# One of three products of a graph layer, moved from the node stage into the scoring stage

## The chip, the cores and the metric

The kernel runs on 1 core of one Trainium2 chip. The metric is device time in microseconds of one execution, the median of several runs. Everything is float32.

## What is computed

Four graph layers over 50,000 nodes and 50,000 edges, 256 features. Every layer begins with `h = relu(layernorm(x))`. The change lies in the third one:

```python
h = jnp.maximum(_layernorm(x, axis=-1), 0.0)
x = x + _L2_gnn_ref(h, src, dst, W_s, W_t, W_attn, W_fc, b_fc)

proj_s = feature @ W_s.T                 # feature is h
proj_t = feature @ W_t.T
z = proj_s[src] + proj_t[dst]
z = jnp.where(z >= 0, z, NEG_SLOPE * z)
e = (z @ W_attn.T)[:, 0]
... softmax of e over the edges of one source gives alpha
msg = feature[src] * alpha[:, None]
agg = jax.ops.segment_sum(msg, dst, num_segments=n)
return agg @ W_fc.T + b_fc
```

The kernel multiplies by `W_fc` first: `h @ W_fc.T` for every node goes to memory as the table `h2`, and the last stage of the layer gathers rows of `h2` and sums them. So three products leave the node stage: by `W_s` (table `from_src`), by `W_t` (`to_dst`) and by `W_fc` (`h2`).

## The kernel before

The program is a row of stages, each a `Phase` that ends in a barrier of all engines. Of the third layer three stages matter here.

**The node stage** (`node_pass`, layer 2) walks 50,176 padded rows in 98 groups of 4 tiles of 128 rows. For a group: SyncE loads x (L1208); VectorE adds two biases (L1282, L1283), takes mean and variance (L1304, L1308, L1311) and normalizes (L1318); GpSimd takes the inverse root (L1353) and also scatters the sorted source keys (L1361 to L1366, four indirect DMAs); TensorE turns a tile by two transposes (L1413); ScalarE rectifies it into `h_t` (L1463); TensorE multiplies the turned tile by the 768 columns of `w2` (L1435: 512 columns into one PSUM tile, 256 into another, and each float32 product over two halves of the 256 features); ScalarE copies both to `out` (L1481, L1482); SyncE stores four tables (L1229): `from_src`, `to_dst`, `h2` and `own2`, 512 KB each.

Each engine runs its own list of steps, software-pipelined by `pipeline`: a step with lag L works on group c-L in turn c. On VectorE normalize (lag 2) stands ahead of average (lag 0); on SyncE the load (lag 0) stands ahead of the stores (lag 6). Buffers exist for S = 4 groups, so the join of group c waits until all four stores of group c-4 have landed (L1281, semaphore `t_put`). TensorE turns the first tile of the next group before it multiplies the last tile of this one, and that turn waits for `normed` of the next group.

**The scoring stage** (`score_sources`) comes next. GpSimd gathers rows of `from_src` and `to_dst` for every edge (L1555, L1557), two indirect DMAs per tile of 128 edges, 8 in a block of 4 tiles; VectorE adds, bends and reduces them to a score and makes two one-hot operands; TensorE places the score by one matmul per tile (L1613). ScalarE and SyncE have nothing to do in this stage.

**The merge** of the layer follows some stages later and is the first reader of `h2`.

Of the kernel before, what the change touches and what calls it, by code (L numbers as in the profile page):

```python
# [12 lines left out]
P = 128  # L13
U = 8
R = 16
BANKS = 8
D = 256
# [719 lines left out]


def tile_rows(table, base, n=G):

    return table[bass.ds(base, n * P), :].rearrange("(g p) f -> p g f", p=P)
# [398 lines left out]
def node_pass(nc, k, layer, x_in, mixed_in=None, tables=()):  # L1140
# [6 lines left out]
    n_put = len(tables)  # L1147
    n_out = {0: D + 3, 1: 2 * D, 2: 3 * D, 3: P + 8}[layer]
    banks = 2 if layer == 2 else 4

# [17 lines left out]
    minus_half = ph.sb("minus_half", [P, G])  # L1168
    h_t = [ph.sb(f"h_t{n}", [P, D]) for n in range(G)]
    out = both("out", {0: [P, 1, G, D + 3], 1: [P, 1, G, D], 2: [P, 3, G, D], 3: [P, 1, G, P + 8]}[layer])  # L1170
    junk = [ph.sb(f"junk{n}", [P, D]) for n in range(2)]
# [20 lines left out]
    with nc.Block() as block:  # L1192
        @block.sync
        def _(sp):
# [15 lines left out]
            def store_tables(q):  # L1210

                if layer == 0:
                    sp.wait_ge(out_made, q.H + 1)
                    parts = [rows_h[q.h][:], pair_h[q.h][:]]
                elif layer == 1:
                    sp.wait_ge(out_made, G * (q.H + 1))
                    sp.sem_inc(turn_sp, 1)
                    sp.wait_ge(raw_made, G * (q.H + 1))
                    parts = [out[q.h][:, 0], own[q.h][:]]
                elif layer == 2:  # L1220
                    sp.wait_ge(out_made, G * (q.H + 1))
# [183 lines left out]
        def _(pe):  # L1405
# [11 lines left out]
            def work(q):  # L1417
# [3 lines left out]
                for g in range(G):  # L1421
# [11 lines left out]
                    for w, (n, matrix) in enumerate(k.products[layer]):  # L1433
                        for c in range(2):
                            ins = nc.tensor.matmul(p_out[w][g % banks][:, 0:n], h_t[g][:, c * P:(c + 1) * P], matrix[:, c, :],  # L1435
                                                   start=c == 0, stop=c == 1)
# [4 lines left out]
        def _(act):  # L1441
# [16 lines left out]
            def rectify(q, g):  # L1458
                t = G * q.H + g
                act.wait_ge(turned, t + 1)  # L1460
                if not q.first:
                    act.wait_ge(product, t - G + 1)
                nc.scalar.activation(h_t[g][:], p_turn[g % 2][:, 0:D], ACT.Relu).then_inc(rectified, 1)  # L1463

            def work(q):
# [3 lines left out]
                for g in range(G):  # L1469
# [10 lines left out]
                    if layer == 2:  # L1480
                        nc.scalar.copy(out[q.h][:, 0:2, g, :], p_out[0][g % banks][:].rearrange("p (n f) -> p n f", n=2))  # L1481
# [32 lines left out]
    ph.close()  # L1514
def score_sources(nc, k, table_src, table_dst, out):

# [10 lines left out]
    at_high = [ph.sb(f"at_high{n}", [P, NT]) for n in range(HOT)]  # L1527
    p_table = ph.ps("table", [P, 512])
    indexed, turn_pool, digits, added, bent, scored, low_hot, high_hot, placed, s_done = (ph.sem(n) for n in (
        "indexed", "turn_pool", "digits", "added", "bent", "scored", "low_hot", "high_hot", "placed", "done"))  # L1530
# [10 lines left out]
    with nc.Block() as block:  # L1541
# [65 lines left out]
        def _(pe):  # L1607
            def tiles(i, first, n):
                for j in range(n):
# [335 lines left out]
def gnn_kernel(nc, a, out, check=None):  # L1945
# [11 lines left out]
    with ExitStack() as ctx:  # L1957
# [15 lines left out]
        def early(name, shape, dt=F32):  # L1973
# [14 lines left out]
        h1, from_src, to_dst, h2, h3 = (dram(n, (k.NP, w)) for n, w in  # L1988
                                        (("h1", D), ("from_src", D), ("to_dst", D), ("h2", D), ("h3", P + 8)))
        mix0, own1, x2, own2, x3 = (dram(n, (k.NP, D)) for n in ("mix0", "own1", "x2", "own2", "x3"))  # L1990

# [36 lines left out]

        node_pass(nc, k, 2, x2, tables=(from_src, to_dst, h2, own2))
        hold = Phase(nc, "soft2")  # L2030
# [9 lines left out]
        score_sources(nc, k, from_src, to_dst, by_place)  # L2040
        shares_by_source(nc, k, by_place, shares)
# [40 lines left out]
```

## Time and profile before

| | us |
|---|---|
| median of 3 runs | 9786.06 |
| lowest, highest | 9783.69, 9792.57 |
| the profiled execution | 9778.72 |
| its span, first to last instruction | 9777.0 |
| node stage of the third layer, in the trace | 4515.6 to 5637.8 |
| scoring stage, in the trace | 5639.1 to 6783.9 |

The profile is one execution. Its engines are PE (TensorE matmuls), PEld (its weight loads), DVE (VectorE), ACT (ScalarE), POOL (GpSimd) and SP (SyncE, which here only issues DMAs). Over the whole span PE is busy 62%, DVE 58%, POOL 50%, ACT 32%; such averages mix stages with different limits, so the stages are read one by one. A float32 matmul of the program stands in the trace as two records.

### The profile page before, as it was taken

The numbers are of one execution on the slowest core, as the hardware profiler recorded it, in microseconds if no ns is written. First come the engines' busy times: TensorE is split into PE (matmuls) and PEld (weight loads), VectorE is DVE, ScalarE is ACT, GpSimd is POOL, SyncE is SP. The second block draws the span as 40 slices with busy tenths as digits, with TensorE's granted clock in tenths as the row PEclk, the third lists the DMA queues.
The fourth block names the chain that finished last, engine by engine and source line by source line (L and its number), as shares of the span: only waits on it lengthen the run. The fifth ranks groups of instructions, "written<-read, shape, count | busy, mean of one in ns | idle before, by whom it ended". The sixth has DMA issues, their size and how long they took to land. (4 is left out here: it accounts for less than half of the span.)

```text
span 9777.0 us, 155051 instructions
## 1 busy us (share of the span) xinstructions
PE 6076.9 (62%) x21338; PEld 3661.3 (37%) x21339; DVE 5653.9 (58%) x19482; ACT 3099.9 (32%) x10799; POOL 4876.5 (50%) x5997
## 2 busy tenths in 40 slices
PE   4666877756768887677999945444003678500277
PEld 3554233324543433455666611111002557400165
DVE  4666988873558776354445455555001458755664
ACT  2665022211554443254444400000000466411046
POOL 1333177756632212664444467775666652455252
PEclk8998577777989998799999966666556999755599
DMA  2332000004876654596666632332002797411057
GB/s 84 134 132 96 0 1 1 1 1 151 284 256 215 214 206 173 181 302 233 236 234 234 222 98 90 91 90 66 1 0 76 234 302 217 144 42 42 23 178 229
DMA packets 779248, 1347.62 MB, mean 138 GB/s; under 512 B 139839, under 2 KB 546391, under 8 KB 779156
## 3 DMA queue, kind: packets, MB, share of 16 engines
q1 hardware_dynamic: 208564, 650.10, 19.0%
q10 hardware_dynamic: 413792, 410.91, 13.2%
q0 software_dynamic: 156800, 285.65, 10.5%
q8 instruction: 25, 0.41, 0.0%
q14 instruction: 67, 0.55, 0.0%
HBM read 751.95 MB, written 594.32 MB: 138 GB/s over the span
## 5 line engine op out<-in xcount | busy, mean ns | idle before, releaser
L1435 PE MATMUL node_p_out<-w,node_h_t 128*128 128x512 f32 (+3 forms) x7840 | 2614.7, 466 | 379.1 <-ACT node_h_t L1463 141.9
L990 PE MATMUL merge_banks<-merge_rows,merge_mask 128*128 x6264 | 1680.7, 425 | 744.0 <-SPq L959 464.5
L1435 PEld LDWEIGHTS node_p_out<-w,node_h_t 128*128 128x128 f32 x7840 | 1357.1, 197 | 1077.7 <-issue 734.9
L990 PEld LDWEIGHTS merge_banks<-merge_rows,merge_mask 128*128 128x128 f32 x6264 | 1278.1, 211 | 1146.6 <-issue 954.0
L972 DVE TENSOR_SCALAR merge_mask<-ramp,dst_at,soft_at_step 128x128 f32<-128x128 f32 x2349 | 847.2, 366 | 1069.8 <-PE merge_banks L990 950.3
L1078 POOL DMA_INDIRECT merge_rows<-h,merge_take_i x1176 | 1125.1, 957 | 655.6 <-issue 249.4
L1022 ACT COPY merge_total<-merge_banks 128x256 f32<-128x256 f32 x1568 | 577.6, 369 | 1251.5 <-PE merge_banks L990 1135.4
L1613 PE MATMUL score_table<-score_at_high,score_at_low 128*128 128x392 f32 x784 | 565.6, 827 | 588.8 <-DVE score_at_high L1574 584.0
L1009 ACT COPY merge_banks<-merge_held 128x256 f32<-128x256 f32 x1568 | 588.1, 376 | 897.5 <-DMA merge_held<-own 643.3
L1353 POOL TENSOR_TENSOR node_inv_std<-node_var,node_minus_half 128x4 f32<-128x4 f32 x392 | 437.0, 1115 | 751.0 <-DVE node_var L1311 750.0
L1463 ACT ACTIVATE node_h_t<-node_p_turn 128x256 f32<-128x256 f32 x1568 | 594.7, 385 | 349.6 <-PE node_p_turn L1413 344.9
L1413 PE MATMUL node_p_turn<-ident,node_xn 128*128 128x128 f32 x3136 | 625.3, 282 | 107.6 <-DVE node_xn L1318 103.8
L1413 PEld LDWEIGHTS node_p_turn<-ident,node_xn 128*128 128x128 f32 x3136 | 439.6, 145 | 444.6 <-issue 232.4
L1613 PEld LDWEIGHTS score_table<-score_at_high,score_at_low 128*128 128x128 f32 x784 | 183.3, 291 | 970.8 <-DVE score_at_low L1588 970.4
L455 POOL DMA_INDIRECT rank_src_of_src<-ends,rank_src_take_src x392 | 371.2, 947 | 340.9 <-ACT rank_src_take_dst L435 228.7
L1660 POOL DMA_INDIRECT score_a<-h,score_take_a x392 | 370.1, 944 | 287.1 <-ACT score_take_a L1636 165.0
L1366 POOL DMA_INDIRECT src_sorted<-node_key,node_key_at x392 | 397.7, 1015 | 179.8 <-issue 94.6
L1375 POOL TENSOR_TENSOR node_small<-node_small,node_half 128x4 f32<-128x4 f32 x98 | 98.8, 1008 | 775.4 <-ACT node_junk L1450 775.4
L1557 POOL DMA_INDIRECT score_b<-to_dst,score_take_b x392 | 413.8, 1056 | 130.3 <-issue 130.3
L1555 POOL DMA_INDIRECT score_a<-from_src,score_take_a x392 | 389.7, 994 | 168.9 <-issue 89.6
L1125 POOL DMA_INDIRECT share_in_got<-shares,share_in_take_i x392 | 372.5, 950 | 170.2 <-issue 79.3
L1585 DVE TENSOR_TENSOR score_z<-score_a,score_b 128x256 f32<-128x256 f32 x392 | 163.9, 418 | 494.9 <-DMA score_b<-to_dst,score_take_b 494.9
(409 smaller groups left out, 9678.3 us busy)
## 6 DMA issues: line engine op xcount, KB each, us to landing
h<-node_out SPq DMA_DIRECT2D x196, 512.0 KB, 5.7
merge_held<-own ACTq DMA_DIRECT2D x196, 512.0 KB, 5.8
x<-merge_total ACTq DMA_DIRECT2D x196, 512.0 KB
node_x<-x SPq DMA_DIRECT2D x196, 512.0 KB, 5.9
node_x<-in_x SPq DMA_DIRECT2D x194, 512.0 KB
h<-node_rows_h SPq DMA_DIRECT2D x98, 512.0 KB, 2.7
merge_held<-h ACTq DMA_DIRECT2D x98, 512.0 KB
mix<-merge_total ACTq DMA_DIRECT2D x98, 512.0 KB
```

What stands on the lines that cost most here:

```text
L972: ins = nc.vector.tensor_scalar(mask[j][:], k.ramp[:, 0:P], columns(k.dst_at, s), columns(weight, s), ALU.is_equal, ALU.mult)
L990: nc.tensor.matmul(banks[:, bass.ds(nc.s_assert_within(at[2 * j + 1], 0, (BANKS - 1) * 512, skip_runtime_bounds_check_because=small), D)], ...
L1009: nc.scalar.copy(bank(q, g), held[q.h][:, g, :]).then_inc(seeded, 1)
L1022: nc.scalar.copy(total[q.h][:, g, :], bank(q, g)).then_inc(kept, 1)
L1078: nc.gpsimd.indirect_dma_start(rows[:, (j + n) * D:(j + n + 1) * D], None, table, bass.IndirectOffsetOnAxis(take_i[:, j + n:j + n + 1], 0) ...
L1353: nc.gpsimd.tensor_tensor(inv_std[q.h][:], var[q.h][:], minus_half[:], ALU.pow).then_inc(std_made, 1)
L1366: nc.gpsimd.indirect_dma_start(k.src_sorted, bass.IndirectOffsetOnAxis(key_at[:, g:g + 1], 0), key[:, g:g + 1], None, bounds_check=k.NP - ...
L1413: ins = nc.tensor.transpose(p_turn[g % 2][:, c * P:(c + 1) * P], xn[q.h][:, g, c * P:(c + 1) * P], k.ident[:])
L1435: ins = nc.tensor.matmul(p_out[w][g % banks][:, 0:n], h_t[g][:, c * P:(c + 1) * P], matrix[:, c, :], start=c == 0, stop=c == 1)
L1463: nc.scalar.activation(h_t[g][:], p_turn[g % 2][:, 0:D], ACT.Relu).then_inc(rectified, 1)
L1557: nc.gpsimd.indirect_dma_start(b[m][:], None, table_dst, bass.IndirectOffsetOnAxis(take_b[:, m:m + 1], 0)).then_inc(got[j // LAG], 16)
L1613: nc.tensor.matmul(p_table[:, 0:NT], at_low[j % HOT][:], at_high[j % HOT][:], start=first and j == 0, stop=False, skip_group_check=True).t ...
```

## The change

- In the node stage the product by the last 256 columns of `w2` goes, and its copy. `out` has two parts instead of three, and the PSUM tiles freed make four banks for the 512-column product instead of two.
- The rectified turned tiles, which lived in four small buffers, are now written into `kept_t`, one of 512 KB for each of the 4 group slots, and the fourth store of a group writes `kept_t` to a new table `turned2` in place of the store of `h2`. Before the first tile of a slot ScalarE waits for that slot's earlier stores.
- In the scoring stage SyncE loads a group of `turned2` (lag 0), TensorE multiplies one tile by the 256 columns right behind each placing matmul, ScalarE copies the result, and SyncE stores a group of `h2` (lag 3). The stage ends when those stores have landed.

```diff
-    n_out = {0: D + 3, 1: 2 * D, 2: 3 * D, 3: P + 8}[layer]
-    banks = 2 if layer == 2 else 4
+    n_out = {0: D + 3, 1: 2 * D, 2: 2 * D, 3: P + 8}[layer]
+    banks = 4
...
+    if layer == 2:
+        kept_t = both("kept_t", [P, G, D])
...
-                    parts = [out[q.h][:, n] for n in range(3)] + [biased[q.h][:]]
+                    parts = [out[q.h][:, n] for n in range(2)] + [biased[q.h][:]]
...
+                if layer == 2:
+                    sp.dma_start(turned_group(tables[3], q.H), kept_t[q.h][:].rearrange("p g f -> p (g f)")
+                                 ).then_inc(t_put[q.h], 16)
...
-                if not q.first:
+                if layer == 2:
+                    if not q.new and g == 0:
+                        act.wait_ge(t_put[q.h], 16 * n_put * q.i)
+                elif not q.first:
                     act.wait_ge(product, t - G + 1)
-                nc.scalar.activation(h_t[g][:], p_turn[g % 2][:, 0:D], ACT.Relu).then_inc(rectified, 1)
+                nc.scalar.activation(turned_rows(q.h, g), p_turn[g % 2][:, 0:D], ACT.Relu).then_inc(rectified, 1)
...
-                        nc.scalar.copy(out[q.h][:, 2, g, :], p_out[1][g % banks][:, 0:D]).then_inc(out_made, 1)
...
+                    side, g = j // G, j % G
+                    if g == 0:
+                        pe.wait_ge(h_got[side], 16 * (i + 1))
+                    if not (first and side == 0):
+                        pe.wait_ge(h_made, t - G + 1)
+                    for c in range(2):
+                        ins = nc.tensor.matmul(p_h[g][:, 0:D], h_t[side][:, g, c * P:(c + 1) * P],
+                                               k.w2[:, c, 2 * D:3 * D], start=c == 0, stop=c == 1)
+                    ins.then_inc(product, 1)
...
+                    if g == 0 and not first:
+                        act.wait_ge(h_put[side], 16 * i)
+                    act.wait_ge(product, i * R + j + 1)
+                    nc.scalar.copy(h[side][:, g, :], p_h[g][:, 0:D]).then_inc(h_made, 1)
...
+            def load(q):
+                if not q.new:
+                    sp.wait_ge(product, G * q.last)
+                sp.dma_start(h_t[q.h][:].rearrange("p g f -> p (g f)"), turned_group(turned_in, q.H)).then_inc(h_got[q.h], 16)
+            def store(q):
+                sp.wait_ge(h_made, G * q.H + G)
+                sp.dma_start(group_rows(h_out, q.H * ROWS), h[q.h][:]).then_inc(h_put[q.h], 16)
+            pipeline(sp, groups, [(0, load), (3, store)], apart=2)
...
-                      2: [(2 * D, k.w2[:, :, 0:2 * D]), (D, k.w2[:, :, 2 * D:3 * D])], 3: [(P + 8, k.w3)], 4: []}
+                      2: [(2 * D, k.w2[:, :, 0:2 * D])], 3: [(P + 8, k.w3)], 4: []}
```

TensorE in the node stage, before, the last two tiles of a group (`p_turn` is the turned tile, `xn` the normalized rows of a slot, `p_out0` and `p_out1` the products of 512 and 256 columns):

```order
L1413 MATMUL node2_p_turn1<-ident,node2_xn0 128x128 x2
L1435 MATMUL node2_p_out0_0<-w2,node2_h_t2 128x512 x2
L1435 MATMUL node2_p_out1_0<-w2,node2_h_t2 128x256 x2
L1413 MATMUL node2_p_turn0<-ident,node2_xn1 128x128 x2
L1435 MATMUL node2_p_out0_1<-w2,node2_h_t3 128x512 x2
L1435 MATMUL node2_p_out1_1<-w2,node2_h_t3 128x256 x2
```

The turn of the next slot's first tile (`xn1`) stands ahead of the product of this group's last tile (`h_t3`).

The same engine and place now:

```order
L1429 MATMUL node2_p_turn1<-ident,node2_xn2 128x128 x2
L1443 REGISTER_ALU
L1448 REGISTER_ALU
L1451 MATMUL node2_p_out0_0<-w2,node2_kept_t2 128x512 x2
L1429 MATMUL node2_p_turn0<-ident,node2_xn2 128x128 x2
L1443 REGISTER_ALU
L1448 REGISTER_ALU
L1451 MATMUL node2_p_out0_1<-w2,node2_kept_t2 128x512 x2
```

The two 256-column matmuls of each tile are gone, and the turned operand is the kept one.

TensorE in the loop of the scoring stage, before (`table` collects the scores):

```order
L1613 MATMUL score2_table<-score2_at_high0,score2_at_low0 128x392
L1611 REGISTER_ALU
L1613 MATMUL score2_table<-score2_at_high1,score2_at_low1 128x392
L1611 REGISTER_ALU
L1613 MATMUL score2_table<-score2_at_high2,score2_at_low2 128x392
```

One placing matmul follows the other, each behind its wait.

The same place now (`h_t1` is a loaded group, `p_h` the product):

```order
L1638 MATMUL score2_table<-score2_at_high1,score2_at_low1 128x392
L1646 MATMUL score2_p_h1<-w2,score2_h_t1 128x256 x2
L1636 REGISTER_ALU
L1638 MATMUL score2_table<-score2_at_high2,score2_at_low2 128x392
L1646 MATMUL score2_p_h2<-w2,score2_h_t1 128x256 x2
```

The two 256-column matmuls stand behind each placing matmul.

SyncE in the loop of the node stage, before, from the load of one group to the wait ahead of the next:

```order
L1208 DMA node_x<-x 128x1024
L1221 ISA
L1229 ISA
L1229 DMA from_src<-node_out 128x1024
L1229 DMA to_dst<-node_out 128x1024
L1229 DMA h<-node_out 128x1024
L1229 DMA own<-node_biased 128x1024
L1207 REGISTER_ALU
```

The four stores of a group stand behind one load, `own` last. The same engine and place now:

```order
L1221 DMA node_x<-x 128x1024
L1234 ISA
L1242 ISA
L1242 DMA from_src<-node_out 128x1024
L1242 DMA to_dst<-node_out 128x1024
L1242 DMA own<-node_biased 128x1024
L1244 ISA
L1244 DMA turned<-node_kept_t 128x1024
L1220 REGISTER_ALU
```

The store of `h` has gone, and one of `turned`, of the same size, stands last.

## Rows read from the trace of the kernel before

**Rows 1.** Busy time by stretch: node stage, scoring stage, an earlier merge.
```profile
4800.00:5200.00 400.00, 400.00 (x1429) 241.61 (x1428) 197.95 (x537) 164.18 (x429) 194.84 (x251) 1.00 0.64 235
5700.00:6200.00 500.00, 251.77 (x347) 81.08 (x347) 285.36 (x1040) 0.00 (x0) 368.18 (x433) 0.66 0.30 91
...
4200.00:4400.00 200.00, 149.48 (x597) 114.52 (x597) 108.18 (x300) 120.73 (x346) 127.68 (x159) 0.96 0.95 309
```

The columns are the stretch, its length in us, and for PE, PEld, DVE, ACT and POOL the busy us (instructions); then TensorE's granted clock as a share of full speed, the share of the DMA engines' time, and GB/s.

**Rows 2.** The 256-column product, node stage: busy us, mean ns, idle before.
```profile
L1435 PE MATMUL node_p_out<-w,node_h_t 128*128 128x256 f32 x1568 | 402.4, 379 | 0.0
```

**Rows 3.** Timeline of one group, node stage: start us, us, instruction, idle before it.
```profile
5099.89 2.75 PE L1435 MATMUL node_p_out<-w,node_h_t 128*128 128x512 f32 x8
...
5102.69 2.75 PE L1435 MATMUL node_p_out<-w,node_h_t 128*128 128x512 f32 x8
...
5103.16 0.38 ACT L1482 COPY node_out<-node_p_out 128x256 f32<-128x256 f32 x1
...
5103.78 0.34 SPq L1229 DMA_DIRECT2D from_src<-node_out  x1
...
5106.91 1.00 SPq L1208 DMA_DIRECT2D node_x<-x  x1
...
5110.92 1.23 DVE L1282 TENSOR_TENSOR node_xc<-node_x,own_bias 128x1024 f32<-128x1024 f32 x1 [5.55 <-DMA own<-node_biased]
...
5114.98 0.33 SPq L1229 DMA_DIRECT2D from_src<-node_out  x1
...
5115.28 1.38 DVE L1318 TENSOR_SCALAR node_xn<-node_xc,node_moments,node_inv_std 128x256 f32<-128x256 f32 x4
```

**Rows 4.** Timeline of the second layer's node stage, whose product has 512 columns.
```profile
3204.84 1.88 PE L1435 MATMUL node_p_out<-w,node_h_t 128*128 128x512 f32 x4
...
3206.78 1.88 PE L1435 MATMUL node_p_out<-w,node_h_t 128*128 128x512 f32 x4
```

**Rows 5.** Half-microsecond stretches of the node stage, columns as in rows 1.
```profile
5106.00:5106.50 0.50, 0.50 (x3) 0.26 (x2) 0.00 (x0) 0.50 (x3) 0.04 (x1) 1.00 1.00 401
...
5111.50:5112.00 0.50, 0.50 (x3) 0.23 (x2) 0.50 (x1) 0.50 (x3) 0.00 (x0) 1.00 0.42 126
```

**Rows 6.** Waits of DVE in the node stage: total us, times, longest.
```profile
DVE node_xc L1282 <- DMA own<-node_biased: 501.2, 94, 6.3
```

**Rows 7.** POOL in one group of the node stage, timeline: first and last instruction.
```profile
5104.21 1.19 POOL L1353 TENSOR_TENSOR node_inv_std<-node_var,node_minus_half 128x4 f32<-128x4 f32 x1 [3.81 <-DVE node_var L1311]
...
5110.39 0.97 POOL L1366 DMA_INDIRECT src_sorted<-node_key,node_key_at  x1 [0.30 <-issue]
```

**Rows 8.** The scatters of POOL in the node stage, all of them.
```profile
L1366 POOL DMA_INDIRECT src_sorted<-node_key,node_key_at x392 | 397.7, 1015 | 179.8 <-issue 94.6 <-POOL node_key L1362 85.2
```

**Rows 9.** POOL in the scoring stage, groups of instructions.
```profile
L1557 POOL DMA_INDIRECT score_b<-to_dst,score_take_b x392 | 413.8, 1056 | 130.3 <-issue 130.3
L1555 POOL DMA_INDIRECT score_a<-from_src,score_take_a x392 | 389.7, 994 | 168.9 <-issue 89.6 <-POOL score_take_b L1551 79.3
```

**Rows 10.** Waits of DVE in the scoring stage.
```profile
DVE score_z L1585 <- DMA score_b<-to_dst,score_take_b: 494.9, 98, 11.3
```

**Rows 11.** One-microsecond stretches of the scoring stage, columns as in rows 1.
```profile
6206.00:6207.00 1.00, 0.00 (x0) 0.00 (x0) 0.27 (x1) 0.00 (x0) 0.88 (x1) 0.50 0.05 16
...
6210.00:6211.00 1.00, 1.00 (x2) 0.38 (x2) 1.00 (x6) 0.00 (x0) 0.91 (x1) 0.50 0.44 131
...
6213.00:6214.00 1.00, 0.89 (x2) 0.30 (x2) 0.31 (x2) 0.00 (x0) 0.70 (x2) 1.00 0.26 94
```

**Rows 12.** Gathers of POOL in the merge at 4200 to 4400 us: ns min/median/max.
```profile
L1078 POOL DMA_INDIRECT merge_rows<-h,merge_take_i x127: 940/946/1032, 4200.1 to 4399.1; - x127
```

**Rows 13.** A gather in the scoring stage's loop, POOL beside busy DVE.
```profile
6223.86 1.30 POOL L1555 DMA_INDIRECT score_a<-from_src,score_take_a  x1 [0.30 <-issue]
```

**Rows 14.** End of the scoring stage, timeline.
```profile
6783.36 0.57 DVE L1604 COPY soft_by_place<-score_table 128x392 f32<-128x392 f32 x1 [1.23 <-PE score_table L1613]
```

**Rows 15.** Landing of the first layer's 512 KB stores.
```profile
DMA to landing us min/median/max: 2.6/2.7/3.3
```

More of the change, by code:

```diff
@@ L736, in pipeline, with turned_group @@
         step(s // S, s % S)
+def turned_group(table, H):
+    return table[bass.ds(H * P, P), :]
 def tile_rows(table, base, n=G):
@@ L1168, in node_pass, with turned_rows @@
     minus_half = ph.sb("minus_half", [P, G])
-    h_t = [ph.sb(f"h_t{n}", [P, D]) for n in range(G)]
-    out = both("out", {0: [P, 1, G, D + 3], 1: [P, 1, G, D], 2: [P, 3, G, D], 3: [P, 1, G, P + 8]}[layer])
+    if layer == 2:
+        kept_t = both("kept_t", [P, G, D])
+    else:
+        h_t = [ph.sb(f"h_t{n}", [P, D]) for n in range(G)]
+    def turned_rows(side, g):
+        return kept_t[side][:, g, :] if layer == 2 else h_t[g][:]
+    out = both("out", {0: [P, 1, G, D + 3], 1: [P, 1, G, D], 2: [P, 2, G, D], 3: [P, 1, G, P + 8]}[layer])
     junk = [ph.sb(f"junk{n}", [P, D]) for n in range(2)]
@@ L1434, in work @@
                         for c in range(2):
-                            ins = nc.tensor.matmul(p_out[w][g % banks][:, 0:n], h_t[g][:, c * P:(c + 1) * P], matrix[:, c, :],
+                            ins = nc.tensor.matmul(p_out[w][g % banks][:, 0:n], turned_rows(q.h, g)[:, c * P:(c + 1) * P], matrix[:, c, :],
                                                    start=c == 0, stop=c == 1)
@@ L1480, in work @@
                     if layer == 2:
-                        nc.scalar.copy(out[q.h][:, 0:2, g, :], p_out[0][g % banks][:].rearrange("p (n f) -> p n f", n=2))
-                        nc.scalar.copy(out[q.h][:, 2, g, :], p_out[1][g % banks][:, 0:D]).then_inc(out_made, 1)
+                        nc.scalar.copy(out[q.h][:, 0:2, g, :], p_out[0][g % banks][:].rearrange("p (n f) -> p n f", n=2)
+                                       ).then_inc(out_made, 1)
                     else:
@@ L1514, in node_pass, with score_sources @@
     ph.close()
-def score_sources(nc, k, table_src, table_dst, out):
+def score_sources(nc, k, table_src, table_dst, out, turned_in, h_out):
     ph = Phase(nc, "score2")
@@ L1528, in score_sources @@
     p_table = ph.ps("table", [P, 512])
+    groups = NT // G
+    h_t = [ph.sb(f"h_t{n}", [P, G, D]) for n in range(S)]
+    h = [ph.sb(f"h{n}", [P, G, D]) for n in range(S)]
+    p_h = [ph.ps(f"p_h{n}", [P, 512]) for n in range(G)]
+    product, h_made = ph.sem("product"), ph.sem("h_made")
+    h_got, h_put = ph.sem_per_slot("h_got", S), ph.sem_per_slot("h_put", S)
     indexed, turn_pool, digits, added, bent, scored, low_hot, high_hot, placed, s_done = (ph.sem(n) for n in (
@@ L1614, in tiles, with _ @@
                                      stop=False, skip_group_check=True).then_inc(placed, 1)
-            in_tiles(pe, tiles)
+                    side, g = j // G, j % G
[7 more added lines that the diff above has]
+                    ins.then_inc(product, 1)
+            in_tiles(pe, tiles)
+        @block.scalar
+        def _(act):
+            def tiles(i, first, n):
+                for j in range(n):
+                    side, g = j // G, j % G
+                    if g == 0 and not first:
+                        act.wait_ge(h_put[side], 16 * i)
+                    act.wait_ge(product, i * R + j + 1)
+                    nc.scalar.copy(h[side][:, g, :], p_h[g][:, 0:D]).then_inc(h_made, 1)
+            in_tiles(act, tiles)
+        @block.sync
+        def _(sp):
+            def load(q):
[6 more added lines that the diff above has]
+            pipeline(sp, groups, [(0, load), (3, store)], apart=2)
+            for side in range(S):
+                sp.wait_ge(h_put[side], 16 * uses_of(side, groups))
     ph.close()
@@ L1989, in gnn_kernel @@
                                         (("h1", D), ("from_src", D), ("to_dst", D), ("h2", D), ("h3", P + 8)))
+        turned2 = dram("turned2", (k.NT // G * P, G * D))
         mix0, own1, x2, own2, x3 = (dram(n, (k.NP, D)) for n in ("mix0", "own1", "x2", "own2", "x3"))
@@ L2027, in gnn_kernel @@
         hold.close()
-        node_pass(nc, k, 2, x2, tables=(from_src, to_dst, h2, own2))
+        node_pass(nc, k, 2, x2, tables=(from_src, to_dst, own2, turned2))
         hold = Phase(nc, "soft2")
@@ L2039, in _ @@
                 nc.vector.memset(by_place[:], 0.0).then_inc(zero, 1)
-        score_sources(nc, k, from_src, to_dst, by_place)
+        score_sources(nc, k, from_src, to_dst, by_place, turned2, h2)
         shares_by_source(nc, k, by_place, shares)
```

## The prediction

> **What bounds the kernel now.** I read the granted clock and busy time by stretch first, then inside the two stages the groups of instructions, the waits, and one group's timeline.
>
> In the node stage TensorE is the bound: in 400 us it is busy 400, at full clock (2.4 GHz), and 1429 records at 40 to a group (4 tiles of 8 product and 2 transpose records) are 35.7 groups, so 11.20 us each [rows 1]. The timeline agrees: stores of one group issue at 5103.78, of the next at 5114.98, and tiles start at 5099.89 and 5102.69, 2.80 us apart [rows 3]. VectorE waits 501.2 us there, 5.3 a group, for the store of `own` to land [rows 6]; that costs nothing as long as TensorE is late anyway. DMA is busy 0.64 of the time [rows 1], or 7.2 us of a group's 11.20.
>
> In the scoring stage GpSimd is the bound. 433 instructions in 500 us at 10 to a block of four tiles are 43.3 blocks, 11.55 us each [rows 1]; 8 of the 10 are gathers of 994 to 1056 ns with about 0.3 us of issue before each [rows 9]. VectorE waits for a gather's data once in every block, 98 times [rows 10]. TensorE is busy half the time at a mean clock of 0.66, DMA 0.30, ScalarE 0 [rows 1].
>
> **The change, node stage.** Removed from each tile: four passes of 256 columns (two matmuls, two records each: 1568 records, 402.4 us of modelled time [rows 2]) and a copy of 0.38 us on ScalarE. What a tile takes without them can be read in the second layer's stage, which has the 512-column product and the same two transposes: starts at 3204.84 and 3206.78, 1.94 us apart [rows 4]. So a tile falls from 2.80 to 1.94, and a group on TensorE from 11.20 to 4 x 1.94 = 7.76 us. 98 groups x 3.44 = 337 us, if nothing else is late.
>
> Something else nearly is: the ring of four slots. Its steps, from the rows of one group [rows 3]: the product of group c-4 ends about 5102.69, its copies end at 5103.54, the first store issues at 5103.78, VectorE starts group c at 5110.92 when `own` has landed (7.14 us after the first issue), and has finished averaging c and normalizing c-1 at 5115.28 + 1.38 = 5116.66 (5.74 us). TensorE then turns group c-1, before its last tile of c-2. That is 13.97 us from product end to normalized. The change takes one copy of 0.38 out of it, 13.6, and I add 0.1 for the signal to TensorE. To the end of the product of c-1 it is then one tile (1.94), four tiles (7.76) and a turn (0.1) more: 23.5 us for three groups, so 7.83 us a group. TensorE's own 7.76 is as good as met.
>
> DMA: the bytes of a group are the same, 5 transfers of 512 KB, since `turned2` takes the place of `h2`, in pieces of the same 4 KB. Stores run at 401 GB/s, and the load behind them is through before 5112, some 8 us after the first issue [rows 3, 5]. About 1 us of that is the start of the first transfer, before which nothing is moved, and the next burst has such a start too, so about 7.2 us of work must fit into 7.83. It does, at 0.92 of capacity instead of 0.64. SyncE issues for 5103.78 to 5107.91, 4.1 us [rows 3], which fits too.
>
> GpSimd: from 5104.21 to 5111.36, 7.15 us a group [rows 7], and the mean scatter of 1015 ns [rows 8] against the 970 shown adds 0.2: 7.4. It fits, with 0.4 to spare. ScalarE's new wait for the slot's stores stands behind one that VectorE has already passed for the same group, and costs nothing; ScalarE had 164 us of work in 143 tiles [rows 1], 1.15 each, and loses 0.38 of it, in a tile of 1.94. The doubled banks only loosen a wait.
>
> Four limits between 7.2 and 7.83 with jitter in each don't give their maximum. The ends are 7.76 (TensorE alone) and 8.8 (GpSimd, below); I take 8.0, close to the measured steps: 98 x (11.20 - 8.0) = 314 us less.
>
> The Trainium skill (GPSIMD Engine Reference, section 1, Specifications) says that GpSimd shares its SBUF interfaces with VectorE and is held up by VectorE's two-port or two-input instructions. The trace bears that out: a gather takes 0.94 us in a merge [rows 12], 1.03 on average in the scoring stage [rows 9] and up to 1.30 where VectorE works [rows 13]. It speaks against this change, since a faster node stage packs VectorE's 5.5 us a group into 8 instead of 11.2.
>
> The skill's page DMA: Bandwidth & Descriptors ("Where 436 GB/s comes from") puts HBM traffic at about 358 GB/s per core. By that the four stores would take 5.9 us instead of 5.2, a third of the difference falls on each group, and the stage would end some 20 us later; the half-microseconds at 401 GB/s [rows 5] speak for the shorter time.
>
> **The change, scoring stage.** Added per tile: four passes of 256 columns on TensorE, which are 2.80 - 1.94 = 0.86 us at full clock and 1.72 at half (1.2 GHz). The placing matmul has two passes of 392 columns; at the same price per column (0.86 us for 1024) that is 0.66, at half clock 1.32. Sum 1.52 or 3.04 us a tile, 6.1 or 12.2 a block against GpSimd's 11.6. The clock is at 0.50 when a burst begins and at 1.00 at its end [rows 11], when TensorE has been busy for a few us; with more work it has less idle time, so the low level will hold for a smaller part. With 4 us of each block at half clock TensorE needs 8 us, and that is hidden. VectorE waits for placings only four tiles back, a whole block, so a TensorE that trails by a tile or two holds nobody.
>
> Queued behind the product's wait for its load are later placings. SyncE loads up to four groups ahead, as each slot is freed, so that wait is over long before. Added on DMA: 1 MB a block, 2.6 us at 400 GB/s beside 3.5 us of gathers, 0.53 of the time. A gather may land later by a transfer, but GpSimd has three blocks of slack before it needs a slot back. ScalarE's copy of 0.4 us a tile and SyncE's two issues a block lie beside idle time. So 0 for the loop; from below 0 too, since nothing of GpSimd's work is taken away.
>
> At the end there is a tail: before, VectorE's copy closes the stage at 6783.93 [rows 14]. Now the last product trails by about 2 us, then a copy of 0.4, the issue, and a landing of 2.7 [rows 15]: +5 us. Later stages read the same tables.
>
> **Sum.** -314 + 5 = -309 us. The profiled execution took 9778.7 and would take 9470; the median of the runs is 9786, which gives 9477.
>
> **The rivals.**
> - *GpSimd or DMA becomes the bound of the node stage.* If each of the four scatters is stretched from 0.97 to the 1.30 of rows 13, GpSimd needs 7.4 + 1.3 = 8.7 to 8.8 us; a DMA ring that never drains would give about the same. For: GpSimd's spare is only 0.4 us, DMA's 0.6. Against: the mean scatter is 1.015. 98 x (11.20 - 8.8) = 235, less the tail 5: 9786 - 230 = 9556. 17%.
> - *TensorE stays at half clock in the scoring stage.* 12.2 us a block instead of 11.6, 98 x 0.6 = 59 us given back: 9536. For: bursts begin at 0.50; against: the clock rises with far less work now. 6%.
> - *The node stage hardly moves,* because the slot ring lengthens with the load on DMA: that would need 3 x 3.3 = 10 us of extra landing. 9786 within 0.2%. Nothing in the rows has it. 2%.
> - *Slower than before: the gathers of the scoring stage pay for the new transfers.* GpSimd is that stage's bound, so each ns on a gather counts 784 times. To eat 309 us each must take 0.39 us more, 1.42 instead of 1.03; at 1.5 us the time would be 9786 - 309 + 784 x 0.47 = 9845. For: DMA load rises from 0.30 to 0.53 and a second queue comes in. Against: at a load of 0.95 [rows 1] gathers take 0.94 us [rows 12]. 4%.
>
> **How the numbers follow.** My forecast, node stage at 7.8 to 8.4 us a group, gets 71%; its own range is 9450 to 9520. The range reported is 9448 to 9570, which takes in the first two rivals. A change within 0.2% (20 us) is about what a measurement of this kernel can't tell from none. Faster by more than that: 71 + 17 + 6 = 94%; within 2%; slower 4%.
>
> **What would show it.** Right: store issues of neighbouring groups in the node stage 7.8 to 8.2 us apart, DMA share about 0.9, TensorE busy over 0.95 at clock 1.00; in the scoring stage GpSimd's gathers at 1.03 us and the span between its ends within 10 us of 1145, TensorE's mean clock above 0.66. Wrong: GpSimd in the node stage waiting for nothing but its own issue, or scatters of 1.2 us (first rival); TensorE without idle time in the scoring stage (second); gathers above 1.1 us there (fourth); VectorE's wait for `own` still over 5 us a group (third).

## The result, and the profile after

The changed kernel takes 9540.05 us, the median of 4 runs (9511.36 to 9549.37), against 9784.88 before: ratio 0.9745, interval 0.9723 to 0.9768, 245 us less. Forecast were 9477 and 309 us less; the range of 9448 to 9570 holds it. The profiled execution took 9511.36, the shortest of the four, 267 us less than the profiled one before.

The two stages by stretch, node stage and scoring stage, in the columns of [rows 1]:

```profile
4700.00:5200.00 500.00, 480.72 (x1459) 223.84 (x1458) 342.45 (x908) 214.95 (x486) 385.89 (x426) 1.00 0.87 318
5400.00:5900.00 500.00, 349.97 (x1025) 236.76 (x1026) 282.06 (x1029) 63.33 (x170) 370.27 (x424) 0.81 0.54 178
```

In the node stage ScalarE now has two records a tile, 486 in 500 us, so 60.75 groups of 8.23 us where [rows 1] gave 11.20. TensorE is busy 0.96 at full clock, DMA 0.87. In the scoring stage TensorE's mean clock rose from 0.66 to 0.81, and GpSimd works off 10 instructions a block as before, 424 in 500 us instead of 433: 11.79 us a block instead of 11.55.

The node stage's store issues, turned groups and VectorE's starts (timeline, answers to [rows 3]):

```profile
5000.20 0.33 SPq L1242 DMA_DIRECT2D from_src<-node_out  x1
...
5007.43 1.23 DVE L1298 TENSOR_TENSOR node_xc<-node_x,own_bias 128x1024 f32<-128x1024 f32 x1 [3.60 <-DMA turned<-node_kept_t]
...
5007.96 0.34 SPq L1242 DMA_DIRECT2D from_src<-node_out  x1
...
5011.79 1.38 DVE L1334 TENSOR_SCALAR node_xn<-node_xc,node_moments,node_inv_std 128x256 f32<-128x256 f32 x4
...
5013.30 0.43 PE L1429 MATMUL node_p_turn<-ident,node_xn 128*128 128x128 f32 x2 [0.40 <-DVE node_xn L1334]
...
5016.34 0.33 SPq L1242 DMA_DIRECT2D from_src<-node_out  x1
```

The stores of two neighbouring groups issue 7.76 us apart where nothing stalls (5000.20 to 5007.96), and 8.38 where TensorE waits for the next group's normalized rows (5007.96 to 5016.34): VectorE could start only when the last store had landed, 7.23 us after the first was issued, ended at 5013.17, and the turn followed at 5013.30. Landing takes as long as before (7.14), though DMA went from 0.64 to 0.87.

Waits of the node stage, total us, times, longest (first two rows VectorE's and TensorE's, the third GpSimd's):

```profile
DVE node_xc L1298 <- DMA turned<-node_kept_t: 215.4, 94, 3.6
...
PE node_p_turn L1429 <- DVE node_xn L1334: 51.2, 47, 22.5
...
POOL node_inv_std L1369 <- DVE node_var L1327: 41.3, 1, 41.3
```

VectorE's wait fell from 5.3 to 2.3 us a group [rows 6]. Such a wait stood after every group before, too, and cost nothing then; that the ring costs time now is said by TensorE, which waits for normalized rows in 47 of 98 groups (before once, at the start). But GpSimd waited for VectorE once in the whole stage, at its start. Its instructions:

```profile
L1382 POOL DMA_INDIRECT src_sorted<-node_key,node_key_at x392 | 403.8, 1030 | 179.8 <-issue 93.1 <-POOL node_key L1378 85.2 <-DVE node_xn L1334 0.9
L1369 POOL TENSOR_TENSOR node_inv_std<-node_var,node_minus_half 128x4 f32<-128x4 f32 x98 | 145.7, 1486 | 42.4 <-DVE node_var L1327 41.3
L1378 POOL COPY node_key<-fields 128x4 f32 x92 | 47.7, 519 | 0.0
```

The scatters hardly changed in this execution (1015 to 1030 ns, [rows 8]), while the inverse root takes 1.49 us and the copy of four keys 0.52 on average. So two limits are met at once, and which binds is what the experiments ask.

The gathers of the scoring stage, and its end (answers to [rows 9, 14]):

```profile
L1582 POOL DMA_INDIRECT score_b<-to_dst,score_take_b x392 | 416.8, 1063 | 130.3 <-issue 124.2 <-DVE score_z L1610 6.1
L1580 POOL DMA_INDIRECT score_a<-from_src,score_take_a x392 | 412.5, 1052 | 168.9 <-issue 89.6 <-POOL score_take_b L1576 79.3
```

```profile
6510.89 0.57 DVE L1629 COPY soft_by_place<-score_table 128x392 f32<-128x392 f32 x1 [3.37 <-PE score_table L1638]
...
6515.96 0.48 DVE L510 MEMSET src_seg_got<- 128x512 f32 x1 [4.50 <-PEq L42]
```

The gathers of `from_src` grew from 994 to 1052 ns, 392 x 0.058 = 23 us, those of `to_dst` from 1056 to 1063, 3 us. From the last gather the end came later too: VectorE waits 3.37 us for the last placing (1.23 before) and 4.50 for the stores of `h2` and the barrier.

The balance of the profiled execution: from VectorE's first row in the node stage to its last copy in the scoring stage 2264.2 us before (4519.7 to 6783.9) and 2002.2 after (4509.3 to 6511.5), 262 less. The node stage gave 98 x (11.20 - 8.21) = 293 (store issues of `own` run from 4530.7 to 5327.0, 97 steps of 8.21). About 30 went back: 26 between the first and the last gather (1131.9 us before, 1158.0 after), 2 from there to the last copy, and the rest between the two loops. The way from that copy to the next stage took 4 more. Another 10 us were gained ahead of the node stage, in stages that the change doesn't touch.

### The profile page after: what moved, and what is told of

Read it like the earlier page. It is cut to its first block and busy times, and to the rows that moved or that the text cites. A ratio compares the mean times of both kernels' runs of the same rounds, so it can differ in the third digit from the quotient of the medians.

```text
span 9509.7 us, 156195 instructions
## 1 busy us (share of the span) xinstructions
PE 5977.7 (63%) x21338; PEld 3705.3 (39%) x21339; DVE 5663.5 (60%) x19482; ACT 3146.4 (33%) x10799; POOL 4992.6 (53%) x5997
## 3 DMA queue, kind: packets, MB, share of 16 engines
q0 software_dynamic: 156800, 285.65, 10.6%
## 5 line engine op out<-in xcount | busy, mean ns | idle before, releaser
L1451 PE MATMUL node_p_out<-w,node_h_t 128*128 128x259 f32 (+2 forms) x4704 | 1531.1, 450 | 379.7 <-ACT node_h_t L1482 139.7
L1451 PEld LDWEIGHTS node_p_out<-w,node_h_t 128*128 128x128 f32 x4704 | 789.8, 201 | 681.3 <-issue 357.8
L1451 PE MATMUL node_p_out<-w,node_kept_t 128*128 128x512 f32 x1568 | 741.5, 595 | 0.0
L1369 POOL TENSOR_TENSOR node_inv_std<-node_var,node_minus_half 128x4 f32<-128x4 f32 x392 | 465.9, 1188 | 389.7 <-DVE node_var L1327 387.6
L1638 PE MATMUL score_table<-score_at_high,score_at_low 128*128 128x392 f32 x784 | 423.9, 630 | 382.4 <-DVE score_at_high L1599 382.4
L1482 ACT ACTIVATE node_h_t<-node_p_turn 128x256 f32<-128x256 f32 x1176 | 437.5, 380 | 322.5 <-PE node_p_turn L1429 317.6
L1580 POOL DMA_INDIRECT score_a<-from_src,score_take_a x392 | 412.5, 1052 | 168.9 <-issue 89.6
L1646 PE MATMUL score_p_h<-w,score_h_t 128*128 128x256 f32 x1568 | 499.9, 451 | 0.0
L1382 POOL DMA_INDIRECT src_sorted<-node_key,node_key_at x392 | 403.8, 1030 | 179.8 <-issue 93.1
L1659 ACT COPY score_h<-score_p_h 128x256 f32<-128x256 f32 x392 | 146.0, 373 | 1040.0 <-PE score_p_h L1646 1040.0
L1582 POOL DMA_INDIRECT score_b<-to_dst,score_take_b x392 | 416.8, 1063 | 130.3 <-issue 124.2
```

The source lines that it names most:

```text
L1369: nc.gpsimd.tensor_tensor(inv_std[q.h][:], var[q.h][:], minus_half[:], ALU.pow).then_inc(std_made, 1)
L1451: ins = nc.tensor.matmul(p_out[w][g % banks][:, 0:n], turned_rows(q.h, g)[:, c * P:(c + 1) * P], matrix[:, c, :], start=c == 0, stop=c == 1)
L1482: nc.scalar.activation(turned_rows(q.h, g), p_turn[g % 2][:, 0:D], ACT.Relu).then_inc(rectified, 1)
L1582: nc.gpsimd.indirect_dma_start(b[m][:], None, table_dst, bass.IndirectOffsetOnAxis(take_b[:, m:m + 1], 0)).then_inc(got[j // LAG], 16)
L1646: ins = nc.tensor.matmul(p_h[g][:, 0:D], h_t[side][:, g, c * P:(c + 1) * P], k.w2[:, c, 2 * D:3 * D], start=c == 0, stop=c == 1)
```

## The experiments

The twelve kernels ran in three batches of four, each on a chip of its own, told apart by the time of the kernel before on it: 10472 us in the first batch, 9785 in the second, 10341 in the third. Ratios are always to the kernel before on the same chip. "The first chip" is below the one of the result, where the kernel before took 9785 us as well.

**node_alone.** The changed node stage with the old scoring stage; the last product is left out, and the merge gathers from another table:

```diff
-        score_sources(nc, k, from_src, to_dst, by_place, turned2, h2)
+        score_sources(nc, k, from_src, to_dst, by_place)
...
-        merge(nc, k, "merge2", own2, x3, table=h2, weight=at_step)
+        merge(nc, k, "merge2", own2, x3, table=from_src, weight=at_step)
```

> The node stage of the changed kernel, with the scoring stage of the one before; the product by the last matrix is left out altogether and the merge gathers from from_src, a table of the same shape, instead. Theory (the node stage gained 98 groups x 3.0 us, the scoring stage gave some 32 us back): about 9785 - 295 = 9490 us, store issues of neighbouring groups 8.2 us apart, gathers of the scoring stage at 994 and 1056 ns as before. Rival (the loss is in the node stage or in later stages, not in the transfers beside the gathers): as the changed kernel, 9510 to 9540.

Measured: 0.9744 (0.9730 to 0.9758), 10208.6 us against 10471.6, 263 us less. That is not comparable with the 0.9745 of the whole change, which was taken on another chip. Stores of `own`, node stage (shortest, median and longest issue in ns, first and last start):

```profile
L1242 SPq DMA_DIRECT2D own<-node_biased x98: 15/738/1982, 5164.7 to 5977.2; - x98
```

97 steps of 8.38 us: the gain of the node stage on this chip is 98 x 2.82 = 277 us. The row of the gathers has 1170 us from first to last with the old scoring stage (5989.5 to 7160.0), where the first chip's profile has 1132, so the stage is slower here by itself. The 9490 us expected were for the first chip and weren't tested. The 8.2 us a group expected, and gathers as before, were missed here: 8.38 us, and 1013 and 1032 ns instead of 994 and 1056.

**score_alone, score_compute, score_transfers.** The old node stage, and beside the old scoring work the new one on x2 with its result in a spare table: all of it; the matmuls and copies alone; the loads and stores alone.

```diff
-        score_sources(nc, k, from_src, to_dst, by_place)
+        score_sources(nc, k, from_src, to_dst, by_place, x2.rearrange("(r g) f -> r (g f)", g=G), spare)
...
# score_compute: no SyncE block, and
-                        ins = nc.tensor.matmul(p_h[g][:, 0:D], h_t[side][:, g, c * P:(c + 1) * P],
+                        ins = nc.tensor.matmul(p_h[g][:, 0:D], k.ident[:],
...
# score_transfers: no product, no copy, and
-                    sp.wait_ge(product, G * q.last)
+                    sp.wait_ge(placed, G * q.last)
...
-                sp.dma_start(group_rows(h_out, q.H * ROWS), h[q.h][:]).then_inc(h_put[q.h], 16)
+                sp.dma_start(group_rows(h_out, q.H * ROWS), h_t[q.h][:]).then_inc(h_put[q.h], 16)
```

> The node stage of the kernel before, and the scoring stage of the changed one, which loads groups of x2 and stores its product to a spare table, so that its work is added and nothing is taken away. Theory: 30 to 35 us slower than before (9815 to 9820), the mean gather of from_src near 1.05 us instead of 0.99, VectorE's bursts starting later against GpSimd's blocks. Rival (the scoring stage's loss comes with the node stage's change, for example from where its tables lie): within 10 us of before.

> As score_alone, but with the matmuls and ScalarE's copies alone: the product is taken of the identity, nothing is loaded for it and nothing stored. Theory (transfers delay the gathers' landing): within 10 us of before, bursts of VectorE starting 0.7 us after the next block of gathers as before. Rival (TensorE holds VectorE or ScalarE's copies disturb the scoring): most of the 30 us, 9805 or more.

> As score_alone, but with the transfers alone: SyncE loads a group of x2 and stores it to a spare table, paced by the placing matmuls; no product, no copy. Theory: 20 to 35 us slower than before, 9805 to 9820, with gathers of 1.05 us. Rival (the compute is what costs): within 10 us of before.

They ran twice, since the chip of 10472 us was unlike the one of the result:

> score_alone again, on another chip: on the first one the whole program took 10472 us before the change and engines idled at issue, so its small differences can't be carried over. Theory (on a chip of 9785 us, the extra work lengthens the stage by 26 us of gathers and 5 us of tail): first to last gather 1158 us, against 1132 in the profile of before; 30 us slower in all. Rival: within 10 us of before.

> score_compute again, on another chip. Theory (transfers move VectorE's bursts against the gathers): 1132 to 1138 us from first to last gather. Rival (TensorE and ScalarE beside the scoring cost it, as the 36 us on the slow chip say): 1150 us or more.

> score_transfers again, on another chip. Theory: 1150 to 1160 us from first to last gather, VectorE's bursts 1.5 us after the next block instead of 0.7. Rival: 1132 to 1138.

The chip of the repetition, 10341 us, was unlike it too. Ratios, and from the profiles the time from the first to the last gather and GpSimd's waits for VectorE ahead of a block (`score_take_a`):

| | ratio | gathers, us | GpSimd waits, us |
|---|---|---|---|
| chip of 10472 us, node_alone: the old scoring stage | | 1170.5 | 35.1 |
| score_transfers | 1.0011 (1.0003 to 1.0020) | 1170.5 | 27.9 |
| score_compute | 1.0052 (1.0037 to 1.0066) | 1206.2 | 67.7 |
| score_alone | 1.0075 (1.0062 to 1.0088) | 1220.1 | 90.7 |
| chip of 10341 us, score_transfers_2 | 1.0021 (1.0011 to 1.0031) | 1152.5 | 13.2 |
| score_compute_2 | 1.0041 (1.0027 to 1.0055) | 1150.7 | 11.5 |
| score_alone_2 | 1.0062 (1.0046 to 1.0079) | 1182.0 | 44.3 |

By the ratios the whole added work costs 64 to 79 us there. Both parts differ from no change (no interval holds 1), the matmuls and copies cost two to five times what the transfers do, and the parts add up to the whole within the intervals. My theory had it the other way round, and fell for these chips.

On the chip of 10472 us the stretches of the gathers say the same as the ratios: nothing for the transfers, 36 us for the matmuls and copies, 50 for all. On the chip of 10341 us they don't: both parts alone stand at 1151 to 1153 us, inside what was expected for the transfers and for the compute rival at once, and there is no profile of the old stage to set them against; only together do they cost some 30 us more.

What a chip of 10341 us does beside the matmuls can be seen in score_alone_2 (waits of 6300 to 7000 us, TensorE's weight loads and placings, VectorE, GpSimd):

```profile
PEld score_table L1624 <- issue: 102.8, 46, 9.3
...
DVE score_at_low L1599 <- PE score_table L1624: 17.3, 11, 2.5
...
POOL score_take_a L1561 <- DVE score_z L1596: 30.1, 5, 7.7
```

TensorE stands up to 9.3 us at issue, waiting for nothing that the profile shows; in the whole scoring stage of the first chip before the change there was one such wait, of 0.4 us. VectorE then waits for placings and GpSimd for VectorE, which on the first chip GpSimd did not before and hardly does after (6.1 us in all).

The last column of the table follows the stretches: where all the work was added, GpSimd waited some 31 (10341) and 55 us (10472) longer, and the gathers took 30 and 50 us longer. The standing at issue alone does not follow the cost: score_transfers_2, without the products, has more of it in the same window (196.8 us) than score_alone_2, score_compute_2 has 50.1, and node_alone's old stage stands 436.6 us in all. VectorE's waits for placings do follow it (3.1 us in node_alone, 6.4 in score_transfers, 25.9 in score_compute, 68.6 in score_alone). That the matmuls' cost on these chips comes in through VectorE's waiting for them is argued from these rows. What holds the issue is open, and so is the split on a chip of 9785 us, where no such run fell.

What the traces of the first chip do show is where its 26 us sit. The first rows are of the kernel before, the second of the one after: the end of a block's gathers and the start of VectorE's burst.

```profile
6203.84 0.94 POOL L1557 DMA_INDIRECT score_b<-to_dst,score_take_b  x1 [0.30 <-issue]
...
6205.91 0.97 POOL L1555 DMA_INDIRECT score_a<-from_src,score_take_a  x1 [0.81 <-POOL score_take_b L1551]
...
6206.73 0.43 DVE L1585 TENSOR_TENSOR score_z<-score_a,score_b 128x256 f32<-128x256 f32 x1 [4.92 <-DMA score_b<-to_dst,score_take_b]
```

```profile
6008.80 0.94 POOL L1582 DMA_INDIRECT score_b<-to_dst,score_take_b  x1 [0.30 <-issue]
...
6010.87 0.97 POOL L1580 DMA_INDIRECT score_a<-from_src,score_take_a  x1 [0.81 <-POOL score_take_b L1576]
...
6012.59 0.42 DVE L1610 TENSOR_TENSOR score_z<-score_a,score_b 128x256 f32<-128x256 f32 x1 [4.91 <-DMA score_b<-to_dst,score_take_b]
```

The burst began 0.82 us after the next block's first gather, now 1.72; over all 98 blocks the mean went from 0.67 to 1.49. With it VectorE's work falls on other gathers: of the 784, 71 took 1.2 us or more before and 172 after, most of them the fourth to seventh of a block.

That VectorE makes them long shows in the same profiles: gathers with no VectorE instruction beside them took 0.945 us before (208 of them) and 0.953 after (245), none over 0.971, while all others averaged 1.054 and 1.105. The time that gathers share with VectorE is nearly the same (483 and 493 us), so it is the phase and not the amount of VectorE's work that changed.

But the mean start of the burst alone does not fix the cost: own_keys, below, has 1.49 us too, and its gathers take 1148.7 us from first to last, not 1158.0. What moves the burst was not separated on this chip. On the chip of 10341 us, where stalls blur the means, the median start is 0.69 us in score_compute_2 and 0.84 in score_transfers_2, against 0.67 before and 1.38 after on the first chip; so the part of my theory that compute alone leaves the burst in its place held, and the 1.5 us expected of the transfers alone did not come.

**after_again.** The changed kernel on the chip of the next three:

> The changed kernel once more, unaltered, on the chip of this batch, as the base for the other three. Both theories: 0.9745 of the time before if the chip is like the first; on a chip where engines stall at issue the scoring stage is expected to give back more, ratio 0.980.

Measured: 0.9735 (0.9720 to 0.9750), 9533.8 us against 9784.7.

**own_apart.** `own2` is stored by a stage of its own and VectorE waits for that alone:

```diff
+            def store_own(q):
+                sp.wait_ge(bias_in, q.H + 1)
+                sp.dma_start(group_rows(tables[2], q.H * ROWS), biased[q.h][:]).then_inc(own_put[q.h], 16)
...
-                        dve.wait_ge(t_put[q.h], 16 * n_put * q.i)
+                        dve.wait_ge(own_put[q.h], 16 * q.i)
```

> The changed kernel, but own2 is stored as soon as it is made, by a stage of its own, and VectorE waits for that store alone before it joins the slot's next group. Theory (the ring of four slots sets 8.2 us a group: 7.2 us of store landing, 5.9 of VectorE, 11.5 of TensorE to the third group): about 4 us or more leave the ring, TensorE's 7.76 us becomes the bound, and the stage gains 98 x 0.45 = 44 us against the changed kernel, store issues 7.8 us apart. Rival 1 (GpSimd is the bound, it never waits for VectorE's variance in the trace): 8.2 us a group as before. Rival 2 (DMA at 0.87 is the bound): 8.1 or more.

**keys_earlier.** The scatter of the keys stands one layer earlier:

```diff
-                1: [(0, root), (join_lag, deviation)],
-                2: [(0, deviation), (0, keys)],
+                1: [(0, root), (join_lag, deviation), (0, keys)],
```

> The changed kernel, but the scatter of the sorted source keys (GpSimd, four indirect DMAs a group) stands in the second layer's node stage instead of the third's. Theory (GpSimd is not the bound of the third's): the third layer's node stage stays at 8.1 to 8.2 us a group; in the second layer's, where GpSimd idled 7 of 9.9 us, less than 10 us are lost. Rival (GpSimd is the bound): 7.8 to 7.9 us a group, 30 to 40 us gained.

**own_keys.** Both:

> Both together. Theory: no more than own_apart brings, 7.8 us a group, bound by TensorE. Rival (a second limit of GpSimd lies just behind the ring): own_apart alone ends near 8.0 and this one at 7.8.

Stretches of the node stage, in this order: after_again, own_apart, keys_earlier, own_keys.

```profile
4700.00:5200.00 500.00, 467.81 (x1420) 218.21 (x1419) 331.74 (x887) 209.46 (x474) 351.93 (x414) 1.00 0.88 311
```

```profile
4700.00:5200.00 500.00, 489.01 (x1481) 227.39 (x1480) 342.70 (x925) 219.41 (x494) 384.80 (x433) 1.00 0.92 323
```

```profile
4700.00:5200.00 500.00, 484.74 (x1477) 226.98 (x1476) 343.95 (x929) 217.49 (x492) 74.44 (x62) 1.00 0.86 323
```

```profile
4700.00:5200.00 500.00, 500.00 (x1549) 240.48 (x1548) 359.07 (x963) 224.96 (x516) 76.86 (x64) 1.00 0.96 338
```

By ScalarE's records (8 a group) the groups take 8.44, 8.10, 8.13 and 7.75 us. The waits say why; own_apart, then keys_earlier, then own_keys, in the same stretch:

```profile
DVE node_xn L1342 <- POOL node_inv_std L1377: 145.4, 62, 3.1
```

```profile
DVE node_xc L1298 <- DMA turned<-node_kept_t: 136.5, 61, 3.0
...
POOL node_inv_std L1369 <- DVE node_var L1327: 429.1, 62, 7.6
```

```profile
DVE node_xc L1306 <- DMA node_x<-x: 121.5, 65, 3.1
...
POOL node_inv_std L1377 <- DVE node_var L1335: 419.2, 64, 7.6
```

With the ring's long wait gone, VectorE waits in every group for GpSimd's inverse root: GpSimd is then the bound, at 8.10. Its small instructions are as cheap there as before the change (root 1.07 us, copies 0.18), and it is the scatters that grew, to 1257 ns on average. One group of own_apart's timeline shows how:

```profile
5007.40 2.12 POOL L1390 DMA_INDIRECT src_sorted<-node_key,node_key_at  x1 [0.30 <-issue]
...
5007.45 1.22 DVE L1307 TENSOR_TENSOR node_biased<-node_x,both_bias 128x1024 f32<-128x1024 f32 x1
```

Between 4545 and 5290 us, scatters that met neither of VectorE's two additions took 0.97 us (190 of them, at most 0.98), those that met one 1.55 on average (174). after_again, the unaltered kernel, lies between: root 1.20 us, scatters 1127 ns, and GpSimd waits for VectorE's variance in 68 of 98 groups, which it did not in the first profile. So which of GpSimd's instructions pays depends on what stands beside the additions, and that differs between two executions of one kernel.

With GpSimd's key work gone, it idles 6.9 us a group, and the ring holds at 8.13. The two limits may not be independent: from the first store's issue to VectorE's start the ring takes 7.69 us in after_again and 7.05 in keys_earlier (means over groups 10 to 93), as if the scatters slowed the landing too. That is not shown, since the unaltered kernel had 7.24 in the first profile. With both gone TensorE is busy 500 of 500 us and a group takes the 7.75 that its tiles ask for, with DMA at 0.96. So neither theory alone was right: two limits lay side by side, and the rival written for own_keys, a second limit of GpSimd just behind the ring, is what was found.

In time: own_apart 0.9725 (0.9712 to 0.9739), keys_earlier 0.9741 (0.9725 to 0.9758), neither told from after_again; own_keys 0.9697 (0.9684 to 0.9710), 9487.3 us, 46 us under the changed kernel on the same chip and clear of its interval. It is the fastest version, and all its output is computed. keys_earlier loses in the second layer most of what it gains in the third. That layer's stores of `own` run from 2900.4 to 3849.0 in after_again and from 2914.1 to 3876.2 in keys_earlier, 962 instead of 949 us, and the first of them also comes 10 us later after the stage's first load (2857.8 and 2861.3): 24 us in all, where I had expected a loss under 10. The third layer's stage gains 30.

**own_keys_spread.** own_keys with each group's load and store of 512 KB in the scoring stage cut into four of 128 KB:

```diff
-            pipeline(sp, groups, [(0, load), (3, store)], apart=2)
+            pipeline(sp, groups, [stage for g in range(G) for stage in ((0, load(g)), (3, store(g)))], apart=2)
```

> own_keys with the scoring stage's transfers cut into four loads and four stores of 128 KB a group, each issued as its tile comes free. Theory (a burst of 1 MB in the middle of a block delays the landing of gathers): the gathers' stretch falls from 1149 in own_keys towards 1135 us, 9475 us in all. Rival (it is the amount moved, in whatever pieces, or the compute): 1149 or more, since pieces of 1 KB cost more than those of 4 KB.

Measured: 0.9800 (0.9784 to 0.9817), on the chip of 10341 us. Its gathers run for 1215 us (5847.8 to 7062.7), those of score_alone_2 on the same chip for 1182 (6163.8 to 7345.9) with the transfers whole. own_keys itself has no run on this chip; by this comparison the pieces made the stage some 33 us longer, against my theory.

But the gathers themselves were shorter (1021 and 1013 ns against 1031 and 1022); what grew is idle time, with GpSimd waiting 84.5 us for VectorE ahead of a block instead of 44.3, so on this chip the theory on the landing was hardly put to the test. The node stage of own_keys holds here too, with 7.75 us a group. Whether smaller pieces or eight issues more a group did it was not separated.

## Why the prediction came out as it did

**The node stage, TensorE's part.** Right: 2.80 to 1.94 us a tile; groups without a stall are 7.76 us apart, and own_keys runs at 7.75.

**The ring.** The mechanism was right, its size too small by 1.2 us in 23.5. I had 23.5 us for three groups: 7.14 of landing, 5.74 of VectorE, 10.6 from normalized rows to the third group's first store. Over groups 10 to 93 of the profile after, the means are 7.24, 5.95 and 11.47, together 24.7, or 8.22 a group. Most of the difference is in the last part. I read it as a stall in one group that delays the product of the next two, where I had summed the ring as if it ran alone; no run tests that reading.

**GpSimd at 7.4 us.** This step failed. I priced its stretch by rows with an idle VectorE or one that was late. In the first profile the small instructions grew, the root by 0.29 us and the two key copies from 0.18 and 0.20 to 0.42 and 0.52, and GpSimd waited only once, at the start, with 8.21 us a group; in own_apart the scatters grew, to 1.26 us, and 8.10 us a group is what GpSimd takes where it alone binds. The first rival named the right engine and, by own_apart, the right mechanism, and its sign (GpSimd waiting for nothing but its own issue) came; its price of 8.8 was too high. Part of that is a slip in its sum: the 7.4 held 0.2 for the mean scatter already, so scatters of 1.30 make 7.15 + 1.32, or 8.5. The rule of the Trainium skill that I set beside it, GPSIMD Engine Reference, section 1, on the interfaces shared with VectorE, agrees with these rows: VectorE's share went from 0.49 to 0.68, and the instructions that grew are those beside its additions of two tensors.

**DMA.** Right that it did not bind: at 0.96 in own_keys a group still takes 7.75 us. The rate of 358 GB/s that I took from the Trainium skill, DMA: Bandwidth & Descriptors, "Where 436 GB/s comes from", would have made the landing an estimated 0.6 us longer. In the first profile it grew by 0.1, to 7.2 us, but in after_again it was 7.7, so the runs don't decide between the two prices. DMA does enter through the landing, as one part of the ring.

Together I took 8.0 for a group; it was 8.2 in the first profile and 8.4 in after_again. That is 20 to 40 of the 64 us that are missing.

**The scoring stage at +0.** Wrong by about 26 us on the first chip. The cover that I named held: GpSimd never lacked a slot, VectorE was not held by placings, TensorE's clock rose, and GpSimd had slack of blocks. What I left out is that work beside idle engines can still shift the phase of VectorE's bursts against the gathers, and the gathers' own duration depends on what VectorE does at the same moment. The second half is shown by the durations above; the first, which of the added work shifts the bursts, is not. [rows 13] had shown the 1.30 us. The fourth rival had the place right at a fourteenth of its size: 0.03 us a gather, not 0.47. The argument against it, 0.94 us at a DMA load of 0.95 [rows 12], came from a stage in which VectorE does other work. That the total lies well inside the range owes nothing to this step: the stretch between the gathers' ends grew by 26 us, where I had named 10 as the most.

**The tail at +5.** About right: the last product trailed as expected, copy to next stage took 4.5 us instead of 1.0, and the copy itself came 2 us later.

**The second and third rivals** did not happen: TensorE's clock was 0.81 in the scoring stage, and the node stage moved.

## What to carry to other kernels

When one engine's work shrinks by a third, write down the period of every other engine and of every slot ring beside the new one, and expect to land above the highest when several lie within a few per cent; then take two limits away together, since here each alone changed the time by less than the runs can tell. Price the instructions of an engine that shares its way with another one by their duration while the other is busy, the short ones too. Work put beside an idle engine is not free if it shifts another engine's work against that of the one that sets the pace.

## What was not expected of the hardware

- The same kernel took 9785 us on two chips and 10472 and 10341 us on two others, in 4 to 17 runs each that agree within 0.3%. The old node stage was the same on the three of them that have a profile of it (TensorE busy 500 of 500 us with 1784 to 1787 matmuls); weight loads stood up to 9.3 us at issue in the scoring stage of score_alone_2.
- A copy of 128 x 4 keys on GpSimd took 0.18 us in one group and 1.18 in the next, where it met VectorE's addition of two tensors. The scatter of own_apart above is the same case: 0.97 us became 2.12.

```profile
5008.58 1.22 DVE L1299 TENSOR_TENSOR node_biased<-node_x,both_bias 128x1024 f32<-128x1024 f32 x1
...
5008.66 1.18 POOL L1378 COPY node_key<-fields 128x4 f32 x1
```
